# Cross attention: keys and queries projected one batch sooner, values moved to a batch's beginning

## The reference, cut to what matters

```python
qp = q @ Wq.T                                  # q: 8 x 256 x 512, 16 heads of 32
kv = latent_kv @ Wkv_expand.T                  # latent_kv: 8 x 256 x 128
k, v = jnp.split(kv, 2, axis=-1)
scores = einsum('bhqd,bhkd->bhqk', qh, kh) / sqrt(32)
attn = softmax(where(causal, scores, min))
out = einsum('bhqk,bhkd->bhqd', attn, vh).reshape(b, sq, H) @ Wout.T
x = layernorm(x + out)
```

## Time and profile before

| | us |
|---|---|
| median of 3 runs | 1069.53 |
| lowest and highest | 1067.64, 1072.2 |
| span of the profiled execution | 1071.8 |
| batches 0 to 7 of the cross attention in it | 315.6 to 539.4 |
| batch 0 | 24.9 |
| batch 1, with all the fillings | 30.2 |
| batch 6, which projects nothing | 26.2 |

### The profile page before, as it was taken

The page is one execution under the profiler, slowest core; times in us unless marked ns, Lnnn a source line. Parts: engine busy times, 40 slices in busy tenths (PEclk is TensorE's granted clock), DMA queues, the critical chain, the costliest instruction groups (busy, mean ns, idle before and its releaser), DMA issues. The chain is left out here.

```text
span 1071.8 us, 18099 instructions
## 1 busy us (share of the span) xinstructions
PE 1015.0 (95%) x6368; PEld 857.6 (80%) x6368; DVE 669.3 (62%) x1515; ACT 453.9 (42%) x802; POOL 260.9 (24%) x361
## 2 busy tenths in 40 slices
PE   7899999999979999999879989999999999999997
PEld 5688888888768888887757768889898988778785
DVE  4837556378276677776576827777776775253576
ACT  5523414146135445454543226566656664221110
POOL 4510110104043233333511012312221220503040
PEclk9999999999987999999998989999999999899999
DMA  5503022023787687876721246788788872705042
GB/s 163 190 1 118 0 83 123 0 79 108 197 222 181 190 232 217 235 210 178 265 82 35 82 157 228 252 267 278 245 265 268 259 254 93 228 28 193 3 159 77
DMA packets 87183, 172.66 MB, mean 161 GB/s; under 512 B 8112, under 2 KB 36016, under 8 KB 85328
## 3 DMA queue, kind: packets, MB, share of 16 engines
q1 hardware_dynamic: 81008, 150.08, 45.4%
q0 software_dynamic: 6112, 21.76, 6.1%
HBM read 130.92 MB, written 37.49 MB: 157 GB/s over the span
## 5 line engine op out<-in xcount | busy, mean ns | idle before, releaser
L45 PE MATMUL a_ps_proj<-region_a_rounded,arena 128*128 128x512 f32 x272 | 107.8, 396 | 10.4 <-DVE region_a_rounded L369 6.4
L45 PE MATMUL e_ps_h<-e_x_lo,e_gu_hi 128*128 128x256 f32 (+1 forms) x384 | 110.6, 288 | 3.4 <-DVE e_x_lo L2181 1.3
L962 DVE CUSTOM_DVE_ANT_0 b_dump<-b_ps_s,b_mask 128x128 f32<-128x128 f32 (+1 forms) x256 | 80.3, 353 | 48.2 <-PE b_ps_s L1157 45.0
L46 PE MATMUL e_ps_h<-e_x_hi,e_gu_lo 128*128 128x256 f32 (+1 forms) x384 | 107.4, 280 | 0.0
L47 PE MATMUL e_ps_h<-e_x_hi,e_gu_hi 128*128 128x256 f32 (+1 forms) x384 | 107.4, 280 | 0.0
L47 PE MATMUL a_ps_proj<-region_a_rounded,arena 128*128 128x512 f32 x272 | 106.6, 392 | 0.0
L46 PE MATMUL a_ps_proj<-region_a_rounded,arena 128*128 128x512 f32 x272 | 106.6, 392 | 0.0
L388 DVE SCALAR_TENSOR_TENSOR f_region_b<-a_ps_proj,a_taps,f_region_b 128x510 f32<-128x510 f32 (+2 forms) x96 | 71.6, 746 | 41.7 <-ACT f_region_b L328 39.4
L2187 DVE TENSOR_TENSOR e_gu_lo<-f_region_a,e_gu_hi 128x704 fp32r<-128x704 f32 x92 | 81.4, 886 | 17.1 <-ACT e_gu_hi L2093 16.5
L848 ACT ACTIVATE b_pt<-b_ps_x 128x384 f32<-128x384 f32 x128 | 61.9, 488 | 61.0 <-PE b_ps_x L1181 60.7
L2093 ACT ACTIVATE e_gu_hi<-f_region_a 128x704 fp32r<-128x704 f32 x92 | 72.0, 785 | 31.3 <-PEq L1498 20.2
(11 more groups left out here) (406 smaller groups left out, 2677.2 us busy)
## 6 DMA issues: line engine op xcount, KB each, us to landing
f_region_a<-we_gate_up SPq DMA_DIRECT2D x88, 352.0 KB, 6.2
qk_split<-arena SPq DMA_DIRECT2D x24, 512.0 KB, 5.4
y_slots<-f_region_b SPq DMA_DIRECT2D x16, 512.0 KB, 4.2
f_x_next<-x SPq DMA_DIRECT2D x6, 1024.0 KB, 6.9
b_sk<-qk_split SPq DMA_DIRECT2D x24, 256.0 KB, 4.3
b_sq<-qk_split SPq DMA_DIRECT2D x24, 256.0 KB, 5.8
f_region_a<-we_down SPq DMA_DIRECT2D x12, 512.0 KB, 6.7
f_region_b<-we_down SPq DMA_DIRECT2D x11, 512.0 KB
```

Of the source, the lines that this page charges most:

```text
L45: pe.matmul(out, a_hi, b_lo, start=first, stop=False)
L46: pe.matmul(out, a_lo, b_hi, start=False, stop=False)
L962: ins = dve.tensor_tensor_reduce(dump[:, n % 2, cols], ps_s[:, n % 2, cols], mask[:, cols], -1.0, 3e38, ALU.add, ALU.min, peak[:, u, k, i: ...
```

## The change

`projected(t)` becomes t + 3 throughout: batch 2 ahead of batch 0 as before, batch 3 in batch 0, and so on to batch 7 in batch 4. Batches 5 to 7 project nothing. The next batch's two `value` products go from steps 5 and 6 of unit 1 to step 0 of unit 0. With that the fillings of a batch move: on PE the transposes from step 0 to step 1, keys(b, 0) from step 2 to 3, the queries one step later in both units; on ACT the context and turned parts, keys(b, 0) and the queries go one or two steps later; likewise on DVE, but keys(b, 1) one step sooner. `split_stored` becomes a pair, one semaphore for each unit, and the waits of `value` and `out` name the new tenants of their banks.

```diff
         def projected(t):
-            return {-1: GB, 0: B}.get(t, t + 2)
+            return t + 3
...
-        def split_count(b, u):
-            return 32 * (2 * (b - GB) + u + 1)
+        def split_count(b):
+            return 32 * (b - GB + 1)
...
             def load_stack(b, u):
                 if b >= GB:
-                    sp.wait_ge(split_stored, split_count(b, max(u, int(b == GB))))
+                    sp.wait_ge(split_stored[u], split_count(b))
                     sp.wait_ge(e_ready, order(b - 2, u, UH - 1) + 1)
...
             def fill(t, u, i):                      # ACT
                 b = projected(t)
                 if u == 0:
+                    if real(t + 1) and i < BT:
+                        values(t + 1, i)
                     if real(b):
-                        if i == 0:
+                        if i == 1:
                             context(b)
+                        if i == 2:
                             turned(b, 0)
-                        if i == 1:
                             turned(b, 1)
-                        if i == 2:
+                        if i == 4:
                             keys(b, 0)
-                        if i == 4:
+                        if i == 6:
                             queries(b, 0)
                 else:
                     if real(b):
                         if i == 0:
                             keys(b, 1)
-                        if i == 4:
+                        if i == 5:
                             queries(b, 1)
-                    if real(t + 1):
-                        if i == 5:
-                            values(t + 1, 0)
-                        if i == 6:
-                            values(t + 1, 1)
...
                     if real(b):                     # DVE, unit 0
-                        if i < 2:
-                            turned(b, i)
-                        if i == 3:
+                        if i in (2, 3):
+                            turned(b, i - 2)
+                        if i == 4:
                             keys(b, 0)
-                        if i == 5:
+                        if i == 6:
                             queries(b, 0)
...
                     if real(b):                     # DVE, unit 1
-                        if i == 1:
+                        if i == 0:
                             keys(b, 1)
-                        if i == 5:
+                        if i == 6:
                             queries(b, 1)
...
             def value(b, k):
                 t = b - 1
-                p = projected(t)
-                if t == 0:
-                    pe.wait_ge(xkq_lo_done, q_count(GB, 1) if k else k_count(GB, 0))
-                elif t >= 1 and k == 0:
-                    pe.wait_ge(out_added, 2 * t)
-                elif t >= 1:
-                    if real(p):
-                        pe.wait_ge(xkq_lo_done, q_count(p, 1))
-                    else:
-                        pe.wait_ge(v_done, 2 * t + 2)
+                p = projected(t - 1)
+                if t >= 2 and k == 0:
+                    pe.wait_ge(out_added, 2 * (t - 1))
+                elif t >= 0 and real(p):
+                    pe.wait_ge(xkq_lo_done, q_count(p, 1) if k else k_count(p, 0))
+                elif t >= 0:
+                    pe.wait_ge(v_done, 2 * t + 2)
...
             def fill(t, u, i):                      # PE
                 b, o = projected(t), t - 1
                 if u == 0:
+                    if real(t + 1) and i == 0:
+                        value(t + 1, 0)
+                        value(t + 1, 1)
                     if real(b):
-                        if i == 0:
+                        if i == 1:
                             turn(b, 0)
                             turn(b, 1)
-                        if i == 2:
+                        if i == 3:
                             keys(b, 0)
-                        if i in (3, 4):
-                            query(b, i - 3)
+                        if i in (4, 5):
+                            query(b, i - 4)
                     if real(o) and i in (5, 6):
                         out(o, 0, i - 5)
                 else:
                     if real(b):
                         if i == 0:
                             keys(b, 1)
-                        if i in (3, 4):
-                            query(b, i - 1)
+                        if i in (4, 5):
+                            query(b, i - 2)
                     if real(o) and i in (1, 2):
                         out(o, 1, i - 1)
-                    if real(t + 1) and i in (5, 6):
-                        value(t + 1, i - 5)
```

More of the change, by code:

```diff
@@ L574, in cross_attention @@
         xkq_lo_done = sem("xkq_lo_done")
-        split_stored = sem("split_stored")
+        split_stored = pair("split_stored")
         stack_loaded = pair("stack_loaded")
@@ L662, in store_k @@
                              split[:, u, KH:KL + 1].rearrange("p s c t -> p s (c t)").bitcast(F32))\
-                    .then_inc(split_stored, 16)
+                    .then_inc(split_stored[u], 16)
             def store_q(b, u):
@@ L824, in keys @@
                 if b > GB:
-                    act.wait_ge(split_stored, split_count(b - 1, u))
+                    act.wait_ge(split_stored[u], split_count(b - 1))
                 act.activation(split[:, u, KH].rearrange("p c t -> p (c t)"), ps_pj[:, u], ACT.Copy).then_inc(xkq_hi_done, 1)
@@ L1135, in out @@
                         pe.wait_ge(out_added, 2 * b + 1)
[L1136 to L1139, removed]
+                    elif real(projected(t)):
+                        pe.wait_ge(xkq_lo_done, k_count(projected(t), 0))
+                    elif real(t + 1):
+                        pe.wait_ge(v_done, 2 * (t + 1) + 1)
                     else:
```

## The result

The changed kernel takes 1079.3 us (median of four runs, 1075.0 to 1081.4), the kernel before 1068.6 in the four beside it: 1.0097 of it, 95% interval 1.0066 to 1.0129. It is slower, by some 10 us or 1.0%. A second set of runs, further down, gives 1.0089 (1.0056 to 1.0123).

A forecast was written before the change was run, and what follows sets the result against it. PE's order was taken to bound batches 1 to 5, with room at both ends. 4.9 + 3.9 - 4.0 - 1.3 + 2.0 = +5.5 us gave 1075.0 on the median (profiled span 1071.8 to 1077.3); range 1065 to 1082.

The forecast's parts named there:

- The gap ahead of keys: Head of batches 1 to 4: keys(b, 0) waits for x_lo's first half, a new gap of 1.6 us.
- The gap ahead of the query: Head of batches 1 to 4: the first query waits for x_lo's second half on DVE, a new gap of 0.45 us.
- The gap at attend: End of batches 1 to 4: ACT drains the last query ahead of exponential 6, so attend waits, new gap 0.4 us.
- The waits that go: Batches 1 to 4: load_peaks wait, 0.5 us, and second value product's with 0.1 at attend, 0.4, vanish; earlier load_stack gives -1.3 overall.
- Sum of batches 1 to 4: New gaps less removed waits, +6.2 us over four batches, less 1.3 from SP's queue: +4.9, bounds -4.9 to +15.
- Batch 0: Takes on a projection: 22.3 us if PE never waits, 28.8 with waits, against 24.9: +3.9, bounds -2.6 to +8.
- half a fall: Batch 0: one fall of the clock, costing some 1.5 us, half hidden by DVE.
- Batches 5 and 6: Batch 5 loses its projection, -4.0 us; values at both heads hide 0.3 each and may avert clock falls, together -1.3.
- The clock: Falls behind new gaps, some 1.5 us each: one in batch 0, half hidden, one in the other four: +2.0, bounds 0 to +9.
- Its one fall in batches 1 to 4: Batches 1 to 4 together: one clock fall behind the new gaps, priced at some 1.5 us.
- The rivals: Clock falls at every gap, 1083 us (0.17); batch 0 at full clock, 1067 (0.10); keys unwaited, 1065 (0.10); nets out, 1070 (0.20).
- The second rival: Batch 0 at full clock: dense matmuls release the throttle, it ends at 22.3 to 23 us; total -2.6, 1067; chance 0.10.

The follow-up runs named there:

- values_late_56: Changed kernel, but in batches 5 and 6 the next batch's values stay in steps 5 and 6 of unit 1: 1.0033 of the kernel before.
- mended_more: mended, with residual rows of batches 0 and 1 loaded at batch 0's end and its last two tiles normalized behind the last exponential: 1.0054 of the kernel before.
- old_steps: Changed kernel with the projection's fillings back in their old steps, new shift kept: 1.0056 of the kernel before.
- values_first: Changed kernel's order inside a batch with the old projected(t), nothing projected in batch 0: 1.0090 of the kernel before.
- mended: Changed kernel with x_hi in step 1, values late in batches 5 and 6, x_lo halves reordered, last query drained behind exponential 6: 0.9986 of the kernel before, 1066.6 us.

## Why the prediction was right, and where its size was off

The direction was right, and so was the mechanism in batches 1 to 4. The sum, 5.5 us, was somewhat low for the profile's 7.0 and about half of the medians' 10. By its steps:

- *The gap ahead of keys.* Forecast 1.6 us and a start at 6.7 us from the batch's first scores; it started at 6.71 (351.98), with a gap of 1.4 by the profile and 1.58 from the pair's end by starts. The 0.15 that the sum had for the semaphores, for which it named no row, is 0.14 here (x_lo ends at 351.84). The experiments show the chain: with x_hi before exponential 2 it is 0.9, with DVE's order mended 0.2.
- *The gap ahead of the query.* Forecast 0.45, measured 0.3.
- *The gap at attend.* Forecast 0.4, measured some 0.35, of which the profile puts down 0.19 to the exponential.
- *The waits that go* went: no wait for load_peaks in batches 1 to 4. load_stack comes 3.5 us sooner against the batch, as forecast (361.3 here, 16.0 us into batch 1; 360.05 before, 19.5 into it), and the load of the peaks behind it, issued at 366.5, lands in time. Sum of batches 1 to 4: forecast +4.9, measured +3.2, since each of them is 1.1 us longer than the old batch 1 and not 1.55.
- *Batch 0.* Forecast +3.9 and half a fall; measured +5.2 with a clock of 0.94 and one fall in it. That its 28.8 came so near is luck. Its waits were of the kinds named but shorter: 0.6 at the bank, 1.4 at keys, none marked at the query, 0.7 at the peaks, 1.2 behind DVE, 0.9 at attend, 4.8 for 6.5. Without them and without the fall (some 1.5, for the stretch from 321.69 to 326.07 against its like in batch 1) the batch has 23.8 us, not 22.3. That it pays for batch 5 and no more is what the two pairs of kernels with and without the shift say.
- *Batches 5 and 6: the step that failed in size.* It took -5.3 us: 0.3 us of each batch's values hidden in the head, and a chance that 1.5 us more of matmuls ahead of the thin stretch might keep the clock up. It looked at the head, where the values go, and not at the end, which they leave. Neither gain came. The values at the head make a batch 0.7 us longer, not 0.3 shorter (25.3 for 24.6 without a fall), and the head still falls: in four of nine such batches, among them batch 6 of both profiles of the changed kernel. What the move costs beyond that is at the end: pairs alone, DVE-bound, and a fall onto attend, which no profile with the values late has. Measured -1.3 in the first profile of the changed kernel and -1.4 in the second, 4 us off, and values_late_56 gives 4.5 of it back.
- *The clock.* It priced a fall at 1.5 us from one query product, and that is what one costs in batch 4 (1.6 and 1.5 above 31.3) and in batch 5 of the second profile, on attend (1.6 above 25.3). The one on attend in the first profile costs twice that, since there the low level lasts from 516.4 to 523.2, twice as long as from 502.7 (the two make batch 6 4.5 us longer than 25.3). Its one fall in batches 1 to 4 was about right: the kernels in which keys waits 1.4 us have four falls in the 17 batches that follow batch 0 and project something, each 1 to 2 us behind the start of keys, while the others have one in 34, behind the 4.4 us of mended_more. The falls on attend it did not foresee.
- *The rivals.* Batch 0 did not end at 22.3 to 23 with dense work in it. By the Trainium skill, TensorE: Matmul & The Clock Gate, section "What's actually happening", activity releases the throttle. The trace agrees in that batch 0's clock rose from 0.66 to 0.94. The second rival had a part right that the forecast weighed too lightly: PE's busy time in batch 0 rose by 2.4 us only (22.9 to 25.3) for 8.3 us of projection at full clock. But its waits and gaps rose by 2.8 (2.0 to 4.8), and batch 5, which gave the 8.3 us up, became only 4.9 shorter, as PE stands idle for 2.6 us of what is left of it. Nor is a higher clock sure: in old_steps the same work ran at 0.80 and the batch took 33.9.

What stays open: the profiled executions differ by 7 us and the medians by 10. The falls are not in the same places from one execution to the next (batch 4 in one profile, not in the other, and batch 7's clock 0.92 in the second), so part of the rest is likely more of them; that was not counted over many executions. Why batch 0 takes 26.7 us in the new order with the old shift (values_first), where nothing is projected in it, and why batch 1 of mended does not come down, is open too.

## What to carry to other kernels

When filling work is moved in an order written out by hand, follow each product through the drains of the engines that must touch it before its consumer, at the place that those drains have in *their* engines' orders: here one exponential in front of one drain was 0.5 us in each batch. Look also at the place that the work leaves: a stretch without it may be thin enough for the clock to fall on what comes next, and what comes next may be the densest part. Work that moves from one batch to another is worth what the giver gets shorter less what the taker gets longer, and neither is the work itself: here 8.3 us of it made one 4.9 shorter and the other 5.2 longer, as both then wait for other engines.

## What the hardware showed beyond what I expected

The clock can fall behind a stretch in which no single wait is longer than a microsecond: ahead of the fall at 516.4 PE was busy for 1.10 us of 1.70, with waits of 0.2 to 0.5. And there is a stretch in which PE was busy throughout and the low level stayed. This window is of the kernel before, in batch 0:

```profile
328.50:331.90 3.40, 3.39 (x14) 3.01 (x14) 2.39 (x16) 2.77 (x6) 1.42 (x4) 0.50 1.13 220
```

PE was busy for 3.39 of 3.40 us at the lower level, with pairs and one value product, and the window behind it was at 0.50 as well, while the query product at 308.29 in the earlier trace rows ran at the lower level and the next one, from 311.68, at the full one. What sets the two apart these runs do not show. The same store of 1024 KB landed 4.9 us after its issue in the kernel before, 9.0 in mended and 8.1 in mended_more. And the same kernel before, on one chip, ran from 1061.3 to 1080.0 us in 32 executions, so single runs say nothing at the size of this change.
